# An earlier second routing batch, another order for the last tiles, and constant products on TensorE in its waits

## The reference

```
x = x + conv(ln_c(x))            # causal depthwise convs of 3, 7, 15 taps, then a 96 -> 32 mix
t = tokens(x)                    # 2048 tokens of 512
n = ln_t(t)
probs = softmax(n @ gate_w.T)    # 8 experts
topk_w, topk_idx = top_k(probs, 2); topk_w /= sum(topk_w)
h = silu(n @ w1[e]) * (n @ w3[e])          # 512 -> 1024
t = t + sum over the 2 experts of topk_w * (h @ w2[e])
```

## Time and profile before

| | before |
|---|---|
| median of three runs | 862.25 us |
| profiled execution, its own time | 862.26 us |
| its span on the core | 860.6 us |
| PE busy | 809.1 us, 94% of the span |
| DVE busy | 354.5 us, 41% |
| ACT busy | 326.8 us, 38% |
| mean granted clock of PE | 0.967 |
| first product of the first expert tile | at 202.23 us |

### The profile page before, as it was taken

How to read it: one execution, slowest core, us unless ns; L and a number is a source line. 1 busy time by engine, 2 the same in 40 slices (tenths; PEclk the granted TensorE clock), 3 DMA queues, 4 the chain that set the end, 5 groups by cost and what they waited for, 6 DMA issues and landing times.

```text
span 860.6 us, 12441 instructions
## 1 busy us (share of the span) xinstructions
PE 809.1 (94%) x3852; PEld 670.5 (78%) x3853; DVE 354.5 (41%) x756; ACT 326.8 (38%) x489; POOL 221.1 (26%) x222
## 2 busy tenths in 40 slices
PE   4999999747999999999999999999999999999994
PEld 3887887646888888888888888888888888888883
DVE  5886657768122531244113512621172152135111
ACT  5873665541121622253125313521262171253211
POOL 4445210001111431133114221411251142142211
PEclk9999999756999999999999999999999999999998
DMA  8001232251811461146213711821273156111121
GB/s 311 14 26 49 83 90 62 76 205 28 314 25 37 147 206 25 24 129 224 37 24 80 273 27 34 303 51 24 34 260 83 37 160 193 24 24 37 26 35 24
DMA packets 35074, 83.19 MB, mean 97 GB/s; under 512 B 3056, under 2 KB 19696, under 8 KB 28912
## 3 DMA queue, kind: packets, MB, share of 16 engines
q1 hardware_dynamic: 26256, 63.18, 20.6%
q0 software_dynamic: 8224, 19.40, 12.1%
q10 hardware_dynamic: 576, 0.39, 0.2%
HBM read 64.88 MB, written 18.09 MB: 96 GB/s over the span
## 4 chain that ended last, share of the span: by engine, by line
PE 90%; DVE 5%; issue 2%; ACT 1%; DMA 1%; POOL 0%; ACTq 0%; DVEq 0%; POOLq 0%
PE bank L653 23%; PE bank L655 23%; PE bank L654 23%; PE bank L669 4%; PE bank L566 4%; PE bank L567 3%; PE bank L568 3%; PE bank L647 2%; PE bank L585 1%; PE bank L631 1%; PE bank L578 1%; DVE wc_lo L760 1%; PE bank L595 0%; DMA mixT<-in_mix 0%; ACT xs L426 0%
## 5 line engine op out<-in xcount | busy, mean ns | idle before, releaser
L653 PE MATMUL bank<-w_hi,xT_hi 128*128 128x512 f32 x576 | 229.6, 399 | 1.5 <-DVE xT_lo L932 1.5
L655 PE MATMUL bank<-w_hi,xT_lo 128*128 128x512 f32 x576 | 226.4, 393 | 0.0
L654 PE MATMUL bank<-w_lo,xT_hi 128*128 128x512 f32 x576 | 225.9, 392 | 0.0
L969 DVE TENSOR_TENSOR h<-bank,h 128x512 f32<-128x512 f32 x72 | 49.8, 691 | 301.6 <-PE bank L655 300.0
L653 PEld LDWEIGHTS bank<-w_hi,xT_hi 128*128 128x128 f32 x576 | 109.1, 189 | 23.6 <-DVE xT_lo L932 1.9
L655 PEld LDWEIGHTS bank<-w_hi,xT_lo 128*128 128x128 f32 x576 | 109.0, 189 | 23.7
L654 PEld LDWEIGHTS bank<-w_lo,xT_hi 128*128 128x128 f32 x576 | 109.2, 190 | 22.0
L497 ACT ACTIVATE h<-bank 128x512 f32<-128x512 f32 x72 | 43.0, 598 | 208.8 <-PE bank L655 208.4
L653 PE MATMUL bank<-w_hi,hT_hi 128*128 128x512 f32 x288 | 118.6, 412 | 0.0
L655 PE MATMUL bank<-w_hi,hT_lo 128*128 128x512 f32 x288 | 112.7, 391 | 0.0
L654 PE MATMUL bank<-w_lo,hT_hi 128*128 128x512 f32 x288 | 112.5, 391 | 0.0
(11 more groups left out here) (138 smaller groups left out, 919.4 us busy)
## 6 DMA issues: line engine op xcount, KB each, us to landing
w_raw<-in_units SPq DMA_DIRECT2D x48, 1024.0 KB, 4.9
out_x<-XT SPq DMA_DIRECT2D x17, 256.0 KB, 2.3
XT<-in_x SPq DMA_DIRECT2D x16, 256.0 KB, 6.6
xn_rows<-xnb SPq DMA_DIRECT2D x16, 256.0 KB, 2.3
xg<-xn_rows,gather_at POOLq DMA_INDIRECT x37, 3.4
out_x<-y,add_at POOLq DMA_INDIRECT x36
taps<-in_taps ACTq DMA_DIRECT2D x2, 160.0 KB, 4.5
mixT<-in_mix ACTq DMA_DIRECT2D x1, 48.0 KB, 4.0
```

What stands on the lines that cost most here:

```text
L653: pe.matmul(B[bank][:], stat_hi, hi, start=start, stop=False)
L654: pe.matmul(B[bank][:], stat_hi, lo, start=False, stop=False)
L655: return pe.matmul(B[bank][:], stat_lo, hi, start=False, stop=stop)
L969: dve.tensor_tensor(h[:, j, :], B[2 * j + 1][:], h[:, j, :], ALU.mult).then_inc(h_out, 1)
```

## The change

Six things are changed together.

1. The second batch has three tiles instead of four, and the third has five. The second batch's `mask_batch`, `count`, `rank_batch` and `hot_rows` come one step earlier.
2. In the steps from 26 on, DVE does `t_stats` ahead of `t_join`, and PE `t_moments` ahead of `logit`; the last tile's moments have a bank of their own.
3. DVE's `low_half(0, 0)` moves from step 24 to behind the steps, and ACT's `high_half(0, 1)` likewise.
4. The transposes write their bank in the order that the logits need, and ACT's copy is flat.
5. `hot_rows` of the last batch moves from ahead of the tile tables to between the two halves of `hot`.
6. `warm(times)` is new: products of two constant matrices, 128 columns wide, into bank 0, which nobody reads at that time. 68 of them stand in seven places of the routing.

```diff
-BATCHES = ((0, 8), (8, 12), (12, NT))
+BATCHES = ((0, 8), (8, 11), (11, NT))
...
 def moment_bank(n):
+    if n == NT - 1:
+        return 6
...
-                act.activation(xnT[n % 2][:].rearrange("p q (b d) -> p b d q", d=D),
-                               B[2 + n % 2][:].rearrange("p (b d q) -> p b d q", d=D, q=NQ),
-                               ACT.Copy).then_inc(xnT_out, 1)
+                act.activation(xnT[n % 2][:].rearrange("p q i -> p (q i)"), B[2 + n % 2][:], ACT.Copy).then_inc(xnT_out, 1)
...
-                for k, freed in ((0, 22), (1, 24)):
-                    if t == freed + 1:
-                        act.wait_ge(step_ps, freed)
-                        high_half(act, 0, k)
-
-            for k in range(2, UNITS):
+                if t == 23:
+                    act.wait_ge(step_ps, 22)
+                    high_half(act, 0, 0)
+
+            for k in range(1, UNITS):
                 high_half(act, 0, k)
...
+                turned = B[2 + n % 2][:].rearrange("p (q b d) -> p b d q", q=NQ, b=NB)
                 for b in range(NB):
-                    ins = pe.transpose(B[2 + n % 2][:, P * b:P * b + P], xnb[n % XB][:, b, :], ident[:])
+                    ins = pe.transpose(turned[:, b, :, :], xnb[n % XB][:, b, :], ident[:])
...
+            def warm(times):
+
+                for _ in range(times):
+                    pe.matmul(B[0][:, 0:P], ident[:], ones[:], start=True, stop=True)
+
             for t in range(STEPS + 3):
+                if t == STEPS + 1:
+                    warm(4)
...
+            warm(2)
             logit(NT - 1)
+            warm(10)
             count(len(BATCHES) - 1)
+            warm(25)
 
             for a in range(2 * NT):
+                if a == NT:
+                    warm(5)
...
+            warm(18)
             turn_tokens(1)
+            warm(4)
             pe_tile(0, 1)
...
-                if t == 24:
-                    low_half(dve, 0, 0)
-
+
+            low_half(dve, 0, 0)
             mask_batch(len(BATCHES) - 1)
             rank_batch(len(BATCHES) - 1)
-            hot_rows(len(BATCHES) - 1)
...
             for k in range(2):
+                if k == 1:
+                    hot_rows(len(BATCHES) - 1)
```

More of the change, by code:

```diff
@@ L608, in _ @@
                     x_moments(t + 2)
+                if t >= STEPS:
+                    for n in posts(t - 1):
+                        t_moments(n)
                 for n in posts(t - 3):
                     logit(n)
-                for n in posts(t - 1):
-                    t_moments(n)
+                if t < STEPS:
+                    for n in posts(t - 1):
+                        t_moments(n)
                 for g, (_, stop) in enumerate(BATCHES):
@@ L829, in hot_rows @@
                 pairs, n = slice(2 * first, 2 * stop), 2 * (stop - first)
-                for p in range(first // 2, stop // 2):
+                for p in range(first // 2, -(-stop // 2)):
                     dve.wait_ge(acc_st[p % 4], 16 * (p // 4 + 1))
@@ L860, in _ @@
                     add_conv(p)
+                if t >= STEPS:
+                    for n in posts(t):
+                        t_stats(n)
                 for n in posts(t - 1):
                     t_join(n)
-                for n in posts(t):
-                    t_stats(n)
+                if t < STEPS:
+                    for n in posts(t):
+                        t_stats(n)
                 for n in posts(t - 1):
```

## The result

| | before | after |
|---|---|---|
| median of six runs each, side by side | 862.28 us (861.5 to 864.46) | 865.94 us (863.56 to 866.41) |
| mean of the same runs | 862.83 us | 865.46 us |
| profiled execution, its own time | 862.26 us | 866.41 us |
| its span | 860.6 us | 864.7 us |
| PE busy | 809.1 us | 825.9 us |

The ratio is 1.0032, with a 95% interval from 1.0018 to 1.0046: the changed kernel is 1.6 to 4.0 us slower. The forecast was 864.7 us, in a range of 859.0 to 867.6. Two of all executions, one of the kernel before and one of a variant, took 939 us at a mean clock of 0.829 and are left out everywhere.

A forecast was written before the change was run, and what follows sets the result against it. PE, busy for 94% of the span, bounds the kernel, through gaps and its slower clock up to the turning of `h`. Terms 5.2 - 1.4 + 0.8 - 1.0 + 1.6 - 0.5 - 2.3 = +2.4 on 862.3 give 864.7 us, range 859.0 to 867.6.

The forecast's parts named there:

- early second batch, at the last residual: Ahead of step 25: PE waits for the masks, its clock falls, DVE takes up the last group +5.2 us late.
- last tile's order, to the last logits: Last residual to last logits: ranks and hot rows off the path, shorter copies, high clock, together -1.4 us.
- count to slots: `warm(10)`, fifth tile, `hot_rows`: Last logits to slots: constant products delay the count, +0.8; fifth tile +0.2 and 1.22 of `hot_rows` off the path, -1.0.
- slots to `src_i`: Routing after the slots: the second sixteen wait for DVE, which is not faster itself; 0, at best -0.3 us.
- `src_i` to first product: `warm(18)`, transposes: Around the gather: half of a possible constant-product delay, +1.6 us, and four transposes at the higher clock, -0.5.
- first tile: First expert tile up to turning of `h`: first products at the high clock, limited by DVE, gain -2.3 us.
- The price of strided writing: Transposes writing in strides: taken as nothing, at most +0.4 us for each of 16 tiles.
- The one-hot columns: Path to the first half of the slots: 1.22 us of `hot_rows` leave it.
- rival (c): Constant products in the routing run at the low clock throughout: +8.4, 870.7 us; chance 0.10 with what lies above 866.5.
- Rival (a): Constant products keep the clock up from the last logits on: -1.2, 861.1 us; chance 0.10.
- The bet on half the delay for `warm(18)`: Ahead of the gathered tile: hidden at the high clock, +3.2 us at the low one; half taken, +1.6.
- Rival (b): Clock never falls ahead of step 25 and constant products hold it: -4.5, 857.8 us; chance 0.13 with partial forms.

The follow-up runs named there:

- part 4 alone: Only the transposes' write order and ACT's flat copy changed, against the kernel before: 860.08 us, ratio 0.9972.
- part 5 alone: Only the last batch's `hot_rows` moved between the two halves of `hot`, against the kernel before: 860.81 us, ratio 0.9981.

## Why the prediction was right

The prediction held in its mechanism; that its 864.7 lies within 1.3 us of the median is in part luck, as shown at the end of this section. The landmarks after, less 1.89 us, against the trace before, term by term of the sum:

| term | predicted | measured | from |
|---|---|---|---|
| early second batch, at the last residual | +5.2 | +5.1 | 166.31 against 161.19 |
| last tile's order, to the last logits | -1.4 | -1.8 | 178.54 against 175.22 is +3.3 |
| count to slots: `warm(10)`, fifth tile, `hot_rows` | +0.8 - 1.0 | -0.2 | 191.12 against 188.00 is +3.1 |
| slots to `src_i` | 0 | +0.3 | 7.33 against 7.06 us |
| `src_i` to first product: `warm(18)`, transposes | +1.6 - 0.5 | +1.3 | 8.45 against 7.17 us |
| first tile | -2.3 | -2.2 | 13.55 against 15.79 us |
| sum | +2.4 | +2.4 | 220.45 against 218.02 |

Behind the turning of `h`, 642.4 us are left after and 642.6 before, so the rest of the kernel moved as one block, as assumed.

**The early batch.** This step held in its parts. Less the 1.89 us, the count started at 156.57 (predicted 156.6), the convolution at 158.30 (158.5), the residual at 166.31 (166.4). What the prediction only inferred, that the clock falls in the wait, is in the row of 157 to 160 us, and the chain from the turning through ACT's copy, the deviation and the rank batch is in the brackets of 7.22 and 4.24 us. That it is the place of the count with its ranks, and not the sizes of the batches, is shown: moving them back gave 9.0 us in the medians and 6.4 in the traces. That the clock is one part of it is shown too: holding it gave back 3.7 us, 2.9 in the traces. What is left between these two runs, 3.6 us in the traces, is the wait and the queues behind it. One point was missing: the prediction compared with the residual at 161.19, and did not say that DVE could have come earlier once the weight block was gone. So the early count cost more in the changed kernel (5.8 and 6.4 us in the traces) than in the kernel before (4.8 us in the trace, 3.7 between the medians).

**The last tile's order.** Predicted -1.4, measured -1.8; the excess is not from the parts that the prediction counted. In the changed kernel without constant products the same stretch, from the last residual to the last logits, is 1.34 us shorter than before. The other 0.46 came with them: behind `warm(4)` the granted clock was 1.00 from 172 to 174 us and four transposes took 0.66 us, without it 0.50 (170 to 172 us) and 1.12 us. The prediction gave the constant products nothing here. Its two copies, counted with 1.0 us, gave 0.75 in the trace of part 4 alone. That part gained more elsewhere: about 0.8 us in stage one, where the prediction had asked for a price and not for a gain, and 0.95 us behind the last logits, up to the turning of `h` (215.41 us), where no fall of the clock followed the 84-column products. The copy is not shown to cause the last: the trace of part 5 alone has the old copy and lacks that fall too. The price of strided writing was taken as nothing, and is nothing.

**The one-hot columns.** Predicted -1.2, measured -1.09 us in the trace of part 5 alone and -1.5 us in its median.

**The constant products and the fifth tile.** From the last logits to the slots the sum of -0.2 was right by opposite errors: `warm(10)` delayed the count by 1.46 us instead of the assumed 0.8, and the fifth tile took 0.1 us in the picking and 0.3 in the ranks instead of 0.2 together; but from the start of the count to DVE's taking it up 0.8 us were saved at the higher clock (1.12 against 1.95 us), which was no term of the forecast's sum. The products ran low at the start as assumed, and brought the clock up: rival (c), low throughout, fell. Rival (a) fell because the clock stayed low through `warm(10)`. The bet on half the delay for `warm(18)` came out: the gathered tile was turned 1.8 us late against the predicted 1.6, since the clock came back only at about 205.4 us. Against the same kernel without them, the traces give the constant products -0.5 us up to the last logits, +0.5 to the slots, +0.3 to `src_i`, +1.3 to the first product and -0.9 in the first tile: +0.7 us in all. Over the whole kernel they were worth nothing (866.29 without, 865.94 with).

**Rival (b)**, the clock up ahead of step 25, did not happen by itself. The experiment that forced it came out at 862.28 (at the turning of `h` 0.4 us early), not at the 857.8 of the rival. Its forecast had added gains behind step 25 that the constant products did not give.

**The executions.** The sum gives 864.7, the median was 865.94. The profiled execution took 866.41 us, 4.15 more than the one before: +2.4 of the sum, +1.9 ahead of the weights of step 25, and -0.2 behind the turning of `h`. The 1.89 us by which the trace was late at step 25 can be followed back by the weights of the steps: 1.08 us at the start of the steps, before any changed instruction has run (between -0.7 and +0.7 in the other traces); -0.8 us from the flat copies in stage one; and about +1.6 us at the first batch's count. Busy time by stretch, after:

```profile
139.00:140.40 1.40, 0.24 (x2) 0.24 (x3) 1.26 (x6) 0.00 (x0) 0.00 (x0) 1.00 0.59 169
140.50:143.90 3.40, 3.40 (x12) 2.93 (x12) 1.73 (x10) 0.00 (x0) 0.00 (x0) 0.50 0.27 77
```

The changed kernel without constant products, whose instructions are the same up to there:

```profile
140.50:143.90 3.40, 3.40 (x18) 2.79 (x17) 1.59 (x6) 1.60 (x5) 0.00 (x0) 1.00 0.23 63
```

The clock fell in one and not in the other. It fell there (PEclk 0.50) too in five further of the fourteen traces, two of them of the kernel before with one part of the change, and not in the other eight. A profile of 857.8 us and one of 854.7 us did not have it, and one of 862.6 us (four tiles, no constant products) did. In three of the six the count of the second batch stood behind step 25; in these three the clock fell once more within that step, and the last residual came 0.6 to 1.6 us later than in the like kernels without that. The means, 862.83 and 865.46 us, differ by 2.6 us; those of the kernel without constant products and of the kernel before in its set by 2.4 (865.24 and 862.88). The executions of the kernel before fall in two groups, 39 from 861.17 to 862.52 us and 36 from 863.51 to 864.91; in the first comparison four of its six were in the lower one and five of the changed kernel's six at 864.64 or above.

So the 3.7 us between the medians are not all the change's. By the traces, one execution of each, it is responsible for +2.4 us that the prediction summed and -0.8 us in stage one that it left out, some 1.7 us together; the rest is which executions the medians fell on. The closeness of 864.7 to 865.94 is to that extent luck. Whether the change makes the fall more frequent stays open.

## What to carry to other kernels

Before a short instruction is moved up in an in-order queue, ask when its input is ready, not when its turn comes: this count cost about 6 us ahead of a convolution and nothing behind it, since the wait idled PE, lowered its clock and held up a transpose on which two other queues stood. A change of six parts deserves to be split: five of these were worth 4 us together, and one line lost them and more. Constant products were worth nothing here as long as they ran past their waits; cut to the waits as the traces show them at both levels of the clock, and with the count in its old place, they belong to a kernel of 855 us. Before two medians are compared, look whether the executions fall in groups: landmarks of the traces showed a loss of 1.7 us where the medians showed 3.7.

## What the runs showed of the hardware

- Permuting in the transposes' write to the bank instead of in ACT's write to SBUF was free on PE (293 against 292 ns) and nearly halved the copy, from 1095 to 597 ns for the same 128x512 elements.
- An fp32 product of 128 columns with a constant is two instructions and took 0.23 us (5.83 us for 25) at the high level and 0.46 us (4.61 us for 10) at the low one, so each instruction steps as the narrow ones do.
- Back-to-back products of 42 columns stayed at 0.50 for 7.02 us, while `warm(10)`, 4.6 us long, was followed by a rise. The Trainium skill's page TensorE: Matmul & The Clock Gate, Part 1, says that activity releases the throttle; the second row agrees with it, the first does not. With 0.24 us idle ahead of the slots the clock stayed at 1.00 through both halves; with 1.62 us it fell at 195.1 us, 2.1 us into unbroken work on PE. What decides between them is not shown.
- The 32 products of 84 columns in the first tile were followed by a fall in three of the six traces without constant products (3.3 us long in the trace before), and in none of the eight with them. Kernels with the same instructions up to the first batch's count had the fall there or not. One trace does not tell what the clock of a stretch is in the next execution.
